# One ring of five unit buffers for maxima and weights in an attention kernel with a gated FFN

## What is computed

```
x = L0_attn_X
xn = _layernorm(x, axis=-1)
s = _L0_attn_ref(xn, L0_attn_Wq, L0_attn_Wk, L0_attn_Wv, L0_attn_Wo)
g = _silu(_L0_ffn_ref(xn, L0_ffn_SU_ug, L0_ffn_SU_dp, L0_ffn_Wscale_ug, L0_ffn_Wscale_dp, L0_ffn_W_up, L0_ffn_W_gate, L0_ffn_W_down))
x = x + s * g
```

```
scores = jnp.einsum('bhqd,bhkd->bhqk', Qr, Kr) * DH ** (-0.5)
causal = jnp.triu(jnp.ones((t, t), dtype=bool), 1)
scores = jnp.where(causal, jnp.finfo(scores.dtype).min, scores)
pattern = jax.nn.softmax(scores, axis=-1)
heads = jnp.einsum('bhqk,bhkd->bqhd', pattern, Vh).reshape(b, t, d)
return heads @ Wo.T
```

## Time and profile before

| | |
|---|---|
| median of 3 executions | 1040.95 us (1030.1 to 1044.01) |
| profiled execution | 1043.81 us, span of instructions 1042.1 us, mean TensorE clock 0.91 |
| busy | PE 887.1 us (85%), DVE 533.0 (51%), ACT 459.1 (44%), POOL 384.0 (37%) |
| DMA | 134.54 MB, mean 129 GB/s; 53.4% of 16 engines' span in SP's queue |
| DMAs that load queries and keys | q_s 36, k_s 36, q_m 24, k_m 24, each 384 KB: 30 units |
| first product of the projection, first score of the attention, end of the last weighing | 44.6, 475.5, 1000.4 us |

### The profile page before, as it was taken

One profiled execution on the slowest core, in us unless ns is written; L12 is line 12 of the kernel. 1 busy time (PEld: TensorE's weight loads), 2 busy tenths in 40 slices (PEclk: granted clock), 3 DMA queues, 4 the chain that ended last, 5 costly groups with the idle time before them and its releaser, 6 DMA issues.

```text
span 1042.1 us, 15762 instructions
## 1 busy us (share of the span) xinstructions
PE 887.1 (85%) x5848; PEld 520.4 (50%) x5848; DVE 533.0 (51%) x808; ACT 459.1 (44%) x661; POOL 384.0 (37%) x457
## 2 busy tenths in 40 slices
PE   4599979999999999985899988999959599699842
PEld 1378757767676777662344434444424244244321
DVE  6743245554646454521577765667736377366101
ACT  2333313232223223232677765557725367356730
POOL 4484626262626363421122213422232322035233
PEclk9899989999999999995799987889969699689976
DMA  6132684135333442337188689758975558786042
GB/s 235 40 109 74 189 174 147 57 116 135 114 102 102 120 123 82 102 102 131 41 162 162 131 185 177 158 125 159 204 169 123 120 110 157 163 176 133 31 139 88
DMA packets 74730, 134.54 MB, mean 129 GB/s; under 512 B 8608, under 2 KB 31008, under 8 KB 74528
## 3 DMA queue, kind: packets, MB, share of 16 engines
q1 hardware_dynamic: 73616, 132.49, 53.4%
q10 hardware_dynamic: 1040, 1.05, 0.3%
HBM read 82.66 MB, written 50.59 MB: 128 GB/s over the span
## 4 chain that ended last, share of the span: by engine, by line
PE 29%; DMA 10%; issue 4%; DVE 4%; ACT 3%; SPq 3%; POOL 2%; POOLq 0%; ACTq 0%; DVEq 0%
PE ps L1037 12%; PE ps L1023 7%; PE ps L107 5%; DMA sums<-scr_heads 3%; DVE mx L1139 3%; DMA spread<-scr_inv 3%; ACT probs L1094 3%; PE ps L1052 2%; PE ps L116 2%; DMA wo_raw<-in_wo 2%; DMA scr_inv<-inverse 2%; SPq L857 1%; POOL o_n L950 1%; SPq L79 1%; DMA xt_in<-in_xt 1%
## 5 line engine op out<-in xcount | busy, mean ns | idle before, releaser
L1094 ACT ACTIVATE probs<-ps 128x1024 f32<-128x1024 f32 (+3 forms) x384 | 293.6, 814 | 175.0 <-PE ps L1023 172.2
L1139 DVE TENSOR_REDUCE mx<-ps 128x1 f32<-128x512 f32 (+1 forms) x480 | 280.5, 631 | 174.1 <-PE ps L116 109.0
L1023 PE MATMUL ps<-q_s,k_s 49*128 49x512 f32 (+3 forms) x768 | 174.0, 445 | 46.6 <-ACT probs L1094 33.1
L941 POOL TENSOR_SCALAR_AFFINE_SELECT probs<-probs 128x256 f32<-128x256 f32 x256 | 102.9, 407 | 300.5 <-ACT probs L1094 297.6
L1037 PE MATMUL ps<-probs,v_ones 128*32 128x512 f32 (+3 forms) x1536 | 178.8, 540 | 0.7 <-ACT o_raw L1100 0.6
L1023 PEld LDWEIGHTS ps<-q_s,k_s 49*128 49x128 f32 x768 | 79.1, 199 | 195.5 <-ACT probs L1094 139.5
L107 PE MATMUL ps<-k_m,q_m 48*128 48x512 f32 (+3 forms) x576 | 143.7, 396 | 30.4 <-DVE mx L1139 25.9
L588 DVE TENSOR_REDUCE mx<-ps 128x2 f32<-128x1024 f32 (+2 forms) x80 | 89.4, 1117 | 90.5 <-PE ps L116 57.3
L351 POOL TENSOR_TENSOR hid_lo<-hid,hid_hi 128x512 fp32r<-128x512 f32 x64 | 82.4, 1288 | 138.1 <-ACT hid_hi L507 138.1
L407 PE MATMUL ps<-xh,wug_hi 128*128 128x512 f32 x256 | 108.1, 422 | 2.6 <-PEq L617 2.6
L107 PEld LDWEIGHTS ps<-k_m,q_m 48*128 48x128 f32 x576 | 77.9, 202 | 57.1 <-DVE mx L1139 41.3
(11 more groups left out here) (95 smaller groups left out, 1034.7 us busy)
## 6 DMA issues: line engine op xcount, KB each, us to landing
scr_qk<-kinds SPq DMA_DIRECT2D x96, 256.0 KB, 3.4
q_s<-scr_qk SPq DMA_DIRECT2D x36, 384.0 KB, 6.7
k_s<-scr_qk SPq DMA_DIRECT2D x36, 384.0 KB, 10.5
q_m<-scr_qk SPq DMA_DIRECT2D x24, 384.0 KB, 7.1
k_m<-scr_qk SPq DMA_DIRECT2D x24, 384.0 KB, 10.4
scr_v<-v_st SPq DMA_DIRECT2D x16, 512.0 KB, 4.7
v_ones<-scr_v SPq DMA_DIRECT2D x16, 512.0 KB, 10.0
scr_heads<-o_raw SPq DMA_DIRECT2D x32, 256.0 KB, 7.8
```

Source lines behind the costliest of these rows:

```text
L941: pool.affine_select(out=v, in_=v, compare_op=ALU.is_ge, fill=0.0, base=0, pattern=[[0, 2], [1, P]], channel_multiplier=-1).then_inc(cut, 1)
L1023: last = pe.matmul(ps[:, S_BANK + 2 * p + e, 0:CH - first(c, j)], sh.k_s[par][rows, p, j * P:(j + 1) * P], sh.q_s[par][rows, p, q0:(c + 1) ...
L1094: act.activation(probs[:, s % RING, p, :, 0:w], ps[:, bank:bank + 2, 0:w], ACT.Exp, scale=SCALE).then_inc(exp_ok, 1)
L1139: dve.tensor_reduce(out, ps[:, turn_bank['tile', v, k, e], 0:n * w].rearrange('p (x k) -> p x k', x=n), axis=AX.X, op=ALU.max).then_inc(ti ...
```

## The change

- `EARLY_UNITS` becomes unit 0 alone: 20 tiles in the projection, from slot 5 of chunk 2, over 120 slots. The 15 other units' 300 tiles go into the attention, steps 1 to 177 (`START, SPAN`).
- `q_m`, `k_m` go. `q_s`, `k_s` become a ring of five (`NBUF`), used by maxima and weights; each unit is loaded once, four units ahead. Units 0 and 1 are loaded in chunk 1 as two units were before, units 2 to 4 at the start of the attention, with six small DMAs that copy the rows of ones into the new buffers.
- Maxima rows are copied at steps 5 and 11 of the unit before.
- Values are stored without the ones (`v_raw`); GpSimd copies them beside the ones in `v_ones` (`take_values`), whose ones are set once, in the preparation.
- `CHAIN` is longer: 6 steps instead of 2 from load to reciprocal, 4 instead of 2 from keep to spread, 5 instead of 3 from spread to scale; sums, inverse, spread and heads are double. The second chunk of a sequence starts 14 steps after the first instead of 12.
- After the steps, VectorE takes both last reciprocals before the gates, and SP issues the last chunk's loads ahead of the spread of chunk 6. The output weights' high part is taken at step 12 instead of 3.

```diff
--- before.py
+++ after.py
...
-EARLY_UNITS = (2, 3, 0, 1)
+EARLY_UNITS = (0,)
 NEARLY = len(EARLY_UNITS)
-turn_of = lambda v: EARLY_UNITS.index(v) if v < NEARLY else v
+NBUF = 5
+loads_to = lambda v: v // NBUF + 1
...
-        self.v_ones = [sb(f'v_ones{i}', [P, TB, HG * VW]) for i in range(2)]
+        self.v_raw = [sb(f'v_raw{i}', [P, TB, HG * DH]) for i in range(2)]
+        self.v_ones = [sb(f'v_ones{i}', [P, TB, HG, VW]) for i in range(2)]
...
-    eng.dma_start(sh.v_ones[v % 2][:, :, :], scr['v'][b, :, :, g * HG * VW:(g + 1) * HG * VW]).then_inc(sh.v_in[v % 2], 16)
-
-
-def load_rows(eng, sh, v, c):
-    eng.wait_ge(sh.shift_ok, QC * turn_of(v) + c + 1)
+    eng.dma_start(sh.v_raw[v % 2][:, :, :], scr['v'][b, g]).then_inc(sh.v_in[v % 2], 16)
+
+
+def take_values(pool, sh, v):
+    pool.wait_ge(sh.v_in[v % 2], 16 * (v // 2 + 1))
+    pool.tensor_copy(sh.v_ones[v % 2][:, :, :, 0:DH],
+                     sh.v_raw[v % 2][:, :, :].rearrange('p t (h d) -> p t h d', d=DH)).then_inc(sh.v_set, 1)
+
+
+def load_rows(eng, sh, q_s, v, c):
+    eng.wait_ge(sh.shift_ok, QC * v + c + 1)
     for e in range(2):
         row = SLOT * e + ROWS
         for p in range(NPAIR):
             h = NPAIR * e + p
             src = sh.shift[TPC * h:TPC * (h + 1), v % 4, c, :]
-            dst = sh.q_s[v % 2][row:row + 1, p, c * CH:(c + 1) * CH]
+            dst = q_s[v % NBUF][row:row + 1, p, c * CH:(c + 1) * CH]
             eng.dma_start(dst.bitcast(F32), src.bitcast(F32)).then_inc(sh.row_in[c][v % 2], 16)
...
-        SPAN = NW * (NCHUNK - 2) - 4
+        START, SPAN = (5, NW * (NCHUNK - 3))
         use_at = {}
         for n in range(len(uses)):
-            slot = n * SPAN // len(uses)
+            slot = START + n * SPAN // len(uses)
             use_at.setdefault((2 + slot // NW, slot % NW), []).append(n)
...
-                eng.dma_start(dst, v_st[:, n].rearrange('p t h d -> p t (h d)')).then_inc(v_out[n], 16)
+                dst = scr['v'][b, :, :, TPC * half + 2 * n:TPC * half + 2 * n + 2, :]
+                eng.dma_start(dst.rearrange('g p t n -> p g (t n)'),
+                              v_st[:, n].rearrange('p g t n -> p g (t n)')).then_inc(v_out[n], 16)
...
             def load_early(v):
-                par = v % 2
-                if v == EARLY_UNITS[0]:
-                    eng.wait_ge(sh.ones_set, 1)
-                if turn_of(v) < 2:
-                    for which in range(2):
-                        eng.wait_ge(qk_out[which], 2 * 6 * 16)
-                else:
-                    eng.wait_ge(et_ok, 2 * (tile_turn(EARLY_UNITS[turn_of(v) - 2], NT - 1) + 1))
-                load_qk(eng, scr, sh.q_s[par], sh.k_s[par], v, sh.qs_in[par])
+                eng.wait_ge(sh.ones_set, 1)
+                for which in range(2):
+                    eng.wait_ge(qk_out[which], 2 * 6 * 16)
+                load_qk(eng, scr, sh.q_s[v], sh.k_s[v], v, sh.qs_in[v])
...
                 if c == 1:
-                    load_early(EARLY_UNITS[0])
-                    load_early(EARLY_UNITS[1])
+                    load_early(0)
+                    load_early(1)
                 store_v(c, 1)
                 if c == 1:
                     for n in range(2):
                         eng.wait_ge(v_out[n], 16 * 2)
                     load_v(eng, scr, sh, 0)
                     load_v(eng, scr, sh, 1)
-                if c == 3:
-                    load_early(EARLY_UNITS[2])
-                if c == 5:
-                    load_early(EARLY_UNITS[3])
                 if c == NCHUNK - 2:
-                    load_rows(eng, sh, EARLY_UNITS[2], 0)
+                    load_rows(eng, sh, sh.q_s, 0, 0)
+            load_rows(eng, sh, sh.q_s, 0, 1)
             store_gate(NCHUNK - 1)
-            load_rows(eng, sh, EARLY_UNITS[2], 1)
-            for half in range(QC):
-                load_rows(eng, sh, EARLY_UNITS[3], half)
             for which in range(2):
                 eng.wait_ge(qk_out[which], 16 * 6 * NCHUNK)
                 eng.wait_ge(v_out[which], 16 * NCHUNK)
                 eng.wait_ge(sh.v_in[which], 16)
-                eng.wait_ge(sh.qs_in[which], 2 * 64)
-                for half in range(QC):
-                    eng.wait_ge(sh.row_in[half][which], 64)
...
+                eng.memset(sh.v_ones[i][:, :, :, :], 1.0)
                 last = eng.memset(sh.k_s[i][:, :, :].bitcast(F32), 1.0)
...
-    START, SPAN = (3, 172)
+    START, SPAN = (1, 177)
     tile_step = lambda v, k: START + (NT * (v - NEARLY) + k) * SPAN // len(LATE)
     tiles_at, rows_at = ({}, {})
...
-    chain_at = {NS * (NG * (b + 1) + c): QC * b + c for b in range(B - 1) for c in range(QC)}
-    chain_at[NS * (NU - 1) + 5] = QC * (B - 1)
-    CHAIN = {'load': 3, 'recip': 5, 'keep': 6, 'spread': 8, 'scale': 11, 'high': 12, 'low': 13,
-             ('piece', 0): 15, ('piece', 1): 18, ('sum', 0): 16, ('sum', 1): 19,
-             ('out', 0): 17, ('out', 1): 20}
+    chain_at = {NS * NG * (b + 1) + 14 * c: QC * b + c for b in range(B - 1) for c in range(QC)}
+    chain_at[NS * (NU - 1) + 4] = QC * (B - 1)
+    CHAIN = {'load': 4, 'recip': 10, 'keep': 11, 'spread': 15, 'scale': 20, 'high': 22, 'low': 22,
+             ('piece', 0): 24, ('piece', 1): 28, ('sum', 0): 25, ('sum', 1): 29, ('out', 0): 27, ('out', 1): 31}
...
-        q_m = [sb(f'q_m{i}', [P, NPAIR, T], F32R) for i in range(2)]
-        k_m = [sb(f'k_m{i}', [P, NPAIR, T], F32R) for i in range(2)]
+        q_s = sh.q_s + [sb(f'q_s{i}', [P, NPAIR, T], F32R) for i in range(2, NBUF)]
+        k_s = sh.k_s + [sb(f'k_s{i}', [P, NPAIR, T], F32R) for i in range(2, NBUF)]
...
-        sums = sb('sums', [P, SUMS])
-        inverse = sb('inverse', [P, SUMS])
-        spread = sb('spread', [P, DC, CH])
-        o_in = sb('o_in', [P, DC, CH])
...
-            def load_max(v):
-                if v >= NEARLY + 2:
-                    eng.wait_ge(tile_ok, 2 * NT * (v - NEARLY - 1))
-                load_qk(eng, scr, q_m[v % 2], k_m[v % 2], v, qm_in[v % 2])
+            def load_unit(v):
+                if v >= NBUF:
+                    eng.wait_ge(scored, NPAIR * NS * (v - NBUF + 1))
+                load_qk(eng, scr, q_s[v % NBUF], k_s[v % NBUF], v, sh.qs_in[v % NBUF])
...
-                if ch:
-                    eng.wait_ge(inv_ok, ch)
-                    eng.wait_ge(scaled, ch)
+                if ch >= 2:
+                    eng.wait_ge(inv_ok, ch - 1)
+                    eng.wait_ge(scaled, ch - 1)
...
             def spread_inverse(ch):
-                eng.wait_ge(inv_out, 16 * (ch + 1))
-                if ch:
-                    eng.wait_ge(scaled, ch)
+                eng.wait_ge(inv_out[ch % 2], 16 * (ch // 2 + 1))
+                if ch >= 2:
+                    eng.wait_ge(scaled, ch - 1)
...
-            load_max(NEARLY)
-            load_max(NEARLY + 1)
+            for v in range(2, NBUF):
+                load_unit(v)
+            for i in range(2, NBUF):
+                for e in range(2):
+                    row = SLOT * e + ROWS
+                    eng.dma_start(k_s[i][row:row + 1, :, :].bitcast(F32), k_s[0][row:row + 1, :, :].bitcast(F32)).then_inc(ones_in, 16)
             eng.dma_start(wo[:, :, :], io['wo'].rearrange('(c p) n -> p c n', p=P)).then_inc(wo_in, 16)
             for g in range(NSTEP):
                 u, s = divmod(g, NS)
-                if s == 0 and 1 <= u < NU - 1:
-                    eng.wait_ge(scored, NPAIR * NS * u)
-                    load_qk(eng, scr, sh.q_s[(u + 1) % 2], sh.k_s[(u + 1) % 2], u + 1, sh.qs_in[(u + 1) % 2])
-                    load_rows(eng, sh, u + 1, 0)
-                if s == 2 and 1 <= u < NU - 1:
-                    eng.wait_ge(pv_ok, NS * u)
-                    load_v(eng, scr, sh, u + 1)
+                if s == 0 and 1 <= u < NU - NBUF + 1:
+                    load_unit(u + NBUF - 1)
+                if s == 5 and u < NU - 1:
+                    load_rows(eng, sh, q_s, u + 1, 0)
+                if s == 5 and u < NU - 2:
+                    eng.wait_ge(sh.v_set, u + 1)
+                    load_v(eng, scr, sh, u + 2)
                 if s == 2 and u:
                     store_heads(u - 1, 1)
                 if s == 6:
                     store_heads(u, 0)
-                if s == 8 and 1 <= u < NU - 1:
-                    load_rows(eng, sh, u + 1, 1)
-                for v, k in tiles_of(g):
-                    if k == NT - 1 and v + 2 < NU:
-                        load_max(v + 2)
+                if s == NS - 1 and u < NU - 1:
+                    load_rows(eng, sh, q_s, u + 1, 1)
                 if at(g, 'load') is not None:
                     load_heads(at(g, 'load'))
                 if at(g, 'keep') is not None:
@@ -920,9 +913,10 @@
                 for o in range(DC):
                     if at(g, ('out', o)) is not None:
                         store_out(at(g, ('out', o)), o)
+            keep_inverse(NCHUNK - 2)
             store_heads(NU - 1, 1)
+            load_heads(NCHUNK - 1)
```

(26 more changed lines are left out.)

81 lines of the change are left out of this document (42 added, 39 removed).

## The result

| | before | after |
|---|---|---|
| median of 4 executions | 1039.9 us (1030.1 to 1044.01) | 994.32 us (987.79 to 1013.9) |
| ratio | | 0.9557, 95% interval 0.948 to 0.9635 |

The kernel is 45.6 us faster; 970 (940 to 1011) was forecast. Some executions show a lower clock than others of the same kernel and take longer, and the ratios in this document leave out the slowest of these.

A forecast was written before the change was run, and what follows sets the result against it. TensorE was taken to set the pace in undisturbed units, with disturbances adding 111 us to the attention. First score at 419, attention 509 and tail 43 gave a span of 971, so 970 us, range 940 to 1011.

The forecast's parts named there:

- Projection: Projection and barrier: tiles out, first tile and barrier bring the attention's start from 475.5 to 419 us.
- Tiles out: Projection: 66 of 88 uses (tiles and transposes) leave, 0.67 us each, -44 us (bounds -37 and -51).
- First tile: Projection: first early tile five slots later no longer waits for its keys, -8 us (bounds -6 and -10).
- Barrier: Between projection and attention: four row DMAs instead of twelve, ahead of the gate store, -4.5 us (bounds -3, -7).
- Steps with tiles: Attention steps: 300 tiles instead of 240, 123 two-tile steps, 473 us instead of 420, +53; pieces 20 us as before.
- rival 1: Attention: two-tile steps cost 0.3 us more each in a row, +36, 1006 us; chance 0.13.
- Division and start: Attention: fewer loads and longer chain cover the division's waits; output weights are hidden at step 12, with 2 us to spare.
- rivals 2 and 4: Attention: stalls stay in part, +35 us, chance 0.12 (2); rows or output weights land late, 90 us, chance 0.05 (4).
- For waits and low clock that remain I take 12: Attention: allowance for remaining waits and low clock, 12 us (bounds 0 and 45).
- +4: Start of the attention: idle time at the barrier lowers the clock for three to four steps, +4 us.
- rival 3: Attention: in steps full of bank waits TensorE's clock falls and stays low, 93 us, 1063 or more; chance 0.04.
- Tail: After the last copy of heads: earlier loads of the last chunk, 43 us (bounds 38 and 46) against 41.7.

The follow-up runs named there:

- two early units: The change with units 0 and 1 early instead of unit 0 alone, 280 tiles in 172 attention steps: 969.03 us, ratio 0.9342.
- its own run: The change with its first early tile at slot 0 of chunk 2 instead of slot 5: 1005.7 us, ratio 0.964.
- single tiles at 0, 1, 4, 5: The change with one tile in steps 0, 1, 4 and 5 of each unit, two in the others: 967.37 us, ratio 0.9319.
- the same placing with two early units: The change with units 0 and 1 early and one tile in steps 0, 1, 4, 5 of each unit: 1046.59 us, ratio 0.974.
- spread placing: Tiles spread over the steps by `START, SPAN`, as in the change, so their pattern shifts from unit to unit; the change: 994.32 us.
- second loading: The change with each unit's queries and keys loaded again at step 4 into buffers nothing reads: 1010.5 us.
- old distances: The change with the division's shorter step distances of the kernel before, for chunks 0 to 5: 1013.95 us.

## Why the prediction held, and where it was off

**Projection: right, 12 us too small.** Measured 68.3 us against 56.5. Tiles out: 0.65 per use by the two early units, 43 for 66 uses, as forecast (44). First tile: 10 instead of 8, shown by its own run. Barrier: 6.2 instead of 4.5. Some 9 us are left. A chunk without tiles took 43.3 us (93.09 to 136.44), where the sum had 44.3; over six chunks that would be 6 of the 9, an estimate. Why such a chunk is faster was not tried; the smaller copies and stores of values, which the sum put at nothing, are one candidate.

**Steps with tiles: right.** 473 + 20 for the pieces stands against 540.9 less what the low clock cost. 0.01 of mean clock is 19.8 us at the low clock over a span of 990, and costs 8.1, so 0.41 per us; a unit of 47.8 against 30.3 us gives 0.37. The 112 us then cost 41 to 46, an estimate, and 495 to 500 are left. A clean unit with eight two-tile and four one-tile steps takes 30.4 us (single tiles at 0, 1, 4, 5), the prediction's step times give 29.9. So two-tile steps in a row did not get dearer by the 0.3 us each of rival 1.

**Division and start: waits right.** ScalarE's part of TensorE's waits fell from 33.1 to 6.0 us, there is no gap above 1.3 us behind the first scores of the attention, and the output weights are in time (rivals 2 and 4: no). Which part of the change took the long stalls away is not shown: with both halves of the division's part undone, GpSimd's waits came back at a third of their size.

**The failed step: "For waits and low clock that remain I take 12", with "+4" for the start.** The attention took 540.9 us, not 509. The low clock costs 41 to 46 us in place of these 16. I had read the low clock of the earlier trace rows as what follows stalls, and in good part it was so in the kernel before: 85 of its 133 us followed the gaps of 10.98 and 12.35 us and two of 10.2 and 10.4. With the stalls gone, the clock falls in steps where TensorE is 73 to 97% busy. Low clock in the attention went only from 133 to 112 us. That is rival 3 in its effect, to a third of its extent: 25 to 30 us beyond the 16, against the 93 that it had for steps that never recover. Its cause, bank waits, is not what most falls follow; they follow stretches with narrow products. Whether these make the clock fall is not shown, since one tile in the narrow steps, which shortens them, kept the mean clock at 0.95 in four of six executions of one kernel and in none of two others.

The Trainium skill ("TensorE: Matmul & The Clock Gate", section "A second HAM failure mode: psum-queue depth-cycling"), which the prediction names for rival 3, tells of a clock that swings because of short idle times from cycling through PSUM banks. The trace agrees that the clock swings with no wait of over 1.3 us. It does not agree on these idle times as what sets off the falls: they are 6.4% of the 3 us ahead of a fall and 6.7% of the other stretches.

**Tail: right.** 44.1 us against 43, by the steps named: 14.65 + 13.5 + 16, where the sum had 15 + 13.5 + 15. No run undid the new order of the tail. The fit from which the prediction got 38 to 39 us is, in the Trainium skill ("DMA: Bandwidth & Descriptors", section "Anatomy of one DMA — SWDGE (gpsimd) path"), one for DMAs issued from GpSimd. These are SyncE's, and the 44.1 us do not agree with it.

The errors of 12 and 32 have opposite signs, hence 994 for 970; that they cancel in part is luck. At the mean clock of the two-early kernel, 0.95, the level of the change gives about 970, an estimate.

## What to carry to other kernels

Before removing stalls to win back the clock, see what the clock does in the steps without stalls: compare kernels at equal mean clock, so that work and clock come apart. Do not compare total waits of kernels whose clocks differ, since an engine at half the clock waits less; compare them within the time at the high clock, or just ahead of the falls. Where side work stands in a bound loop can weigh more than its amount: the same 300 tiles gave medians of 967 or 1056 us by which four steps had one tile. But try each placing in many executions. One kernel gave 966 and 1081 us, and the same placing with two early units gave 1047 where 945 to 972 was expected.

## What was not expected of the hardware

- The clock falls to 1.2 GHz in steps where TensorE is mostly busy, with narrow blocks just ahead, here in 55 of 87 cases in the same step of a unit, and comes back by itself after 3 to 38 us in the kernels with the spread placing.
- It can also stay: 236 us at 1.2 GHz with TensorE 99% busy in the units between, 47.8 us per unit instead of 30.3. One kernel's executions took 966 to 1081 us.
- TensorE's waits for VectorE's banks are not more frequent ahead of a fall (6.4% of 3 us) than elsewhere (6.7%); the columns that it streams are fewer (1.7 and 2.6 per ns).
- The inverse's store of 32 KB took 15.78 us to land with the second loading and the old distances together, at most 11.25 with the second loading alone and 8.32 with the old distances alone. In kernels with neither, but another placing of tiles or blocks, the scaling also waited for the spread, by up to 2.5 us.
